# TensorE's routed-tile loop in turns of sixteen tiles instead of eight, with the first 32 tiles written out

## The reference

```python
x = x + attention(layernorm(x))      # 16 heads' width taken as one head of 1024, causal, scores / sqrt(1024)
h = layernorm(x)                     # 4096 tokens, D = 128
scores = softmax(h @ gate_w.T)       # E = 8 experts
top_scores, sel = top_k(scores, 2)   # each token goes to K = 2 experts
y = silu(h @ w1[e]) * (h @ w3[e]) @ w2[e]   # H = 256, per chosen expert e
x = x + sum over the two choices of score * y
```

## Time and profile before

| what | value |
|---|---|
| median of 3 runs | 320.21 us (319.2 to 321.56) |
| the profiled execution | 322.9 us, of which 321.1 us are the span of the trace |
| routed tiles | from 146 us to 307 us of the span |
| TensorE matmuls busy | 249.1 us (78%) |
| VectorE busy | 205.8 us (64%) |
| GpSimd busy | 181.8 us (57%) |
| mean granted TensorE clock | 0.925 of full speed |

### The profile page before, as it was taken

One profiled execution on the slowest core, in us unless ns is written; L12 is line 12 of the kernel. 1 busy time (PEld: TensorE's weight loads), 2 busy tenths in 40 slices (PEclk: granted clock), 3 DMA queues, 4 the chain that ended last, 5 costly groups with the idle time before them and its releaser, 6 DMA issues.

```text
span 321.1 us, 5987 instructions
## 1 busy us (share of the span) xinstructions
PE 249.1 (78%) x1619; PEld 202.1 (63%) x1620; DVE 205.8 (64%) x944; ACT 127.7 (40%) x348; POOL 181.8 (57%) x230
## 2 busy tenths in 40 slices
PE   0788999989798979875949433998998989888900
PEld 0766788869566768573837322877776778677700
DVE  1758988654897547674738213976766767689705
ACT  1155656463564535271326101434434444334400
POOL 4379933737687825618554774555555555455630
PEclk9999999999999979999778755999999999999965
DMA  7953500101001100104112211244332223567436
GB/s 235 324 168 95 166 2 1 44 25 36 26 34 53 47 15 26 42 2 111 43 52 64 70 58 42 70 107 103 83 82 79 74 75 106 175 197 210 141 108 216
DMA packets 31145, 28.94 MB, mean 90 GB/s; under 512 B 4360, under 2 KB 25872, under 8 KB 31120
## 3 DMA queue, kind: packets, MB, share of 16 engines
q1 hardware_dynamic: 25168, 18.81, 21.2%
q0 software_dynamic: 4352, 9.05, 8.4%
q10 hardware_dynamic: 1600, 0.79, 0.8%
HBM read 16.40 MB, written 12.22 MB: 89 GB/s over the span
## 4 chain that ended last, share of the span: by engine, by line
PE 58%; issue 8%; another core or an unknown queue 8%; DVE 8%; SPq 5%; ACT 5%; DMA 4%; POOL 3%; POOLq 0%; DVEq 0%
PE weighed L586 7%; PE scores L625 6%; PE scores L533 6%; PE mixed L648 6%; PE turned L634 5%; PE scores L627 5%; PE weighed L648 5%; PE turned L560 5%; PE scores L626 5%; PE scores L617 2%; DMA ysb<-L_ffn_w 2%; PE mixed L547 2%; ACT Pr L751 2%; SPq L290 1%
## 5 line engine op out<-in xcount | busy, mean ns | idle before, releaser
L444 POOL DMA_INDIRECT choice_rows<-ysb,ydest x72 | 70.1, 974 | 57.7 <-DVE ysb L1027 36.5
L435 POOL DMA_INDIRECT expert_rows<-rows,slots x64 | 63.1, 986 | 22.0 <-issue 16.6
L757 ACT ACTIVATE sil<-scores 128x256 f32<-128x256 f32 x72 | 27.7, 385 | 83.9 <-PE scores L627 62.7
L625 PE MATMUL scores<-W,xTh 128*128 x72 | 35.9, 499 | 13.0 <-issue 8.2
L586 PE MATMUL weighed<-TL,PT 128*128 128x128 f32 x288 | 39.2, 283 | 2.6 <-DVE X L837 1.6
L1007 DVE CAST xTh<-scores 128x128 fp32r<-128x128 f32 x72 | 20.7, 287 | 32.0 <-PE scores L617 19.0
L634 PE MATMUL turned<-identf,g 128*128 128x128 f32 x144 | 30.0, 292 | 11.8 <-DVE g L1017 8.7
L586 PEld LDWEIGHTS weighed<-TL,PT 128*128 128x128 f32 x288 | 35.7, 197 | 3.0 <-issue 2.9
L533 PE MATMUL scores<-XX,TL 128*128 128x512 f32 (+3 forms) x96 | 36.9, 493 | 0.8 <-ACT TL L737 0.7
L388 POOL TENSOR_TENSOR rstd<-ve,halves 128x1 f32<-128x1 f32 x32 | 19.8, 618 | 28.5 <-DVE ve L850 28.2
L762 ACT ACTIVATE gTs<-turned 128x256 f32<-128x256 f32 x72 | 27.6, 383 | 16.5 <-PE turned L634 12.3
(11 more groups left out here) (138 smaller groups left out, 531.9 us busy)
## 6 DMA issues: line engine op xcount, KB each, us to landing
xt<-expert_rows SPq DMA_DIRECT2D x72, 66.0 KB
XX<-choice_rows SPq DMA_DIRECT2D x16, 256.0 KB
ysb<-L_ffn_w SPq DMA_DIRECT2D x16, 128.0 KB, 2.2
choice_rows<-ysb,ydest POOLq DMA_INDIRECT x72
X<-L_attn_in_features SPq DMA_DIRECT2D x2, 512.0 KB, 8.8
expert_rows<-rows,slots POOLq DMA_INDIRECT x64
out<-X SPq DMA_DIRECT2D x4, 256.0 KB
expert_rows<-padrows SPq DMA_DIRECT2D x1, 528.0 KB
```

What stands on the lines that cost most here:

```text
L435: nc.gpsimd.indirect_dma_start(xs, bass.IndirectOffsetOnAxis(ap=slots[:, u, k:k + 1], axis=0), rows[:, u % ROWS_RING, k, :], None).then_in ...
L444: nc.gpsimd.indirect_dma_start(yb, bass.IndirectOffsetOnAxis(ap=ydest[:, q:q + 1], axis=0), ysb[:, q, :], None).then_inc(y_out[q], 16)
L625: mm(bank[2 + j % 2], xTh[:, j % 2, :], hi, start=True, stop=False)
L757: copy(sil[:, j % 2, :], bank[2 + j % 2][:, 0:H], ACT.Silu).then_inc(sil_rdy, 1)
```

## The change

`weights_of`, `step` and its parts take a turn number r and a place q of 0 to 15 in place of m and j of 0 to 7. TensorE's program becomes: a load of 18 entries (16 and the two before them), tiles 0 to 7, the wait for `place_rdy`, tiles 8 to 15 with the same registers, a load and tiles 16 to 31 written out, the wait for `list_rdy` 2, a loop of two turns of sixteen (32 to 63), and a load of 10 entries with tiles 64 to 71 written out. So there are five loads instead of nine, at tiles 0, 16, 32, 48 and 64; the loads at 8, 24, 40 and 56 are gone, and of six loop turns two are left. The matmuls, their order and the counts waited for stay as they are; the other engines' programs are the same.

```diff
-            def turn_x(m, j):
-
-                pe.wait_ge(xt_in[j], 16 * (m + 1))
+            def turn_x(r, q):
+
+                j, rounds = q % LANES, OUT_LANES // LANES
+                pe.wait_ge(xt_in[j], r * (16 * rounds) + 16 * (q // LANES + 1))
                 nc.tensor.transpose(bank[j % 2][:, 0:P], xt[:, j, 0:D], identf[:, :]).then_inc(xT_mm, 1)
 
-            def up(m, j, w):
-
-                t = m * LANES + j
-                pe.wait_ge(xT_rdy, t + 1)
+            def up(r, q, w):
+
+                pe.wait_ge(xT_rdy, r * OUT_LANES + q + 1)
 
                 hi, lo = W13[:, ds(w * UP, 2 * H)], W13[:, ds(w * UP + 2 * H, 2 * H)]
-                mm(bank[2 + j % 2], xTh[:, j % 2, :], hi, start=True, stop=False)
-                mm(bank[2 + j % 2], xTh[:, j % 2, :], lo, start=False, stop=False)
-                mm(bank[2 + j % 2], xTl[:, j % 2, :], hi, start=False, stop=True).then_inc(h_mm, 1)
-
-            def turn_g(m, j):
-
-                t = m * LANES + j
-                pe.wait_ge(g_rdy, t + 1)
+                mm(bank[2 + q % 2], xTh[:, q % 2, :], hi, start=True, stop=False)
+                mm(bank[2 + q % 2], xTh[:, q % 2, :], lo, start=False, stop=False)
+                mm(bank[2 + q % 2], xTl[:, q % 2, :], hi, start=False, stop=True).then_inc(h_mm, 1)
+
+            def turn_g(r, q):
+
+                pe.wait_ge(g_rdy, r * OUT_LANES + q + 1)
                 for c in range(H // P):
-                    i = nc.tensor.transpose(bank[4 + j % 2][:, c * P:(c + 1) * P], g[:, j % 2, c * P:(c + 1) * P],
+                    i = nc.tensor.transpose(bank[4 + q % 2][:, c * P:(c + 1) * P], g[:, q % 2, c * P:(c + 1) * P],
                                             identf[:, :])
                 i.then_inc(gT_mm, 1)
 
-            def down(m, j, w):
-                t = m * LANES + j
+            def down(r, q, w):
+                t = r * OUT_LANES + q
                 pe.wait_ge(gT_rdy, t + 1)
-                if isinstance(m, int) and m == 0:
+                first_eight = isinstance(r, int) and t < LANES
+                if first_eight:
 
                     wait(pe, y_rdy, t)
                     if t == 0:
                         pe.wait_ge(x1_rdy, N_TILES)
 
                 for c in range(H // P):
-                    i = mm(product_bank(m, j)[:, 0:D], gTs[:, j % 2, c * P:(c + 1) * P],
+                    i = mm((pO if first_eight else bank[6 + q % 2])[:, 0:D], gTs[:, q % 2, c * P:(c + 1) * P],
                            w2_sb[:, ds(w + c * D, D)],
                            start=c == 0, stop=c == H // P - 1)
                 i.then_inc(y_mm, 1)
 
-            def weights_of(m):
+            def weights_of(r, n):
 
                 _, w = nc.values_load_multi_w_load_instructions(
-                    wcol[0:1, ds(m * LANES, LIST0 + LANES)], engines=[pe.engine], min_val=0,
+                    wcol[0:1, ds(r * OUT_LANES + LIST0 - 2, n + 2)], engines=[pe.engine], min_val=0,
                     max_val=(E - 1) * WIDE, skip_runtime_bounds_check_because=IN_RANGE)
                 return w
 
-            def step(m, j, w):
-
-                static, t = isinstance(m, int), m * LANES + j
-                m_is_0 = static and m == 0
-                up(m, j, w[LIST0 + j])
-                if m_is_0 and has_xx(N_TILES + j):
-                    transposes(N_TILES + j)
+            def step(r, q, w):
+
+                def of(q):
+                    return r + q // OUT_LANES, q % OUT_LANES
+                static, t = isinstance(r, int), r * OUT_LANES + q
+                ending = static and t < LANES
+                up(r, q, w[2 + q])
+                if ending and has_xx(N_TILES + t):
+                    transposes(N_TILES + t)
                 if not static or t + 2 < NT:
-                    turn_x(m + (j + 2) // LANES, (j + 2) % LANES)
+                    turn_x(*of(q + 2))
                 if not static or t >= 1:
-                    turn_g(m + (j - 1) // LANES, (j - 1) % LANES)
+                    turn_g(*of(q - 1))
                 if not static or t >= 2:
-                    down(m + (j - 2) // LANES, (j - 2) % LANES, w[LIST0 + j - 2])
-                if m_is_0 and has_tl(N_TILES + j):
-                    projections(N_TILES + j)
-                if m_is_0 and group_at(N_TILES + j, RANK_LAG) is not None:
-                    ranks(group_at(N_TILES + j, RANK_LAG))
+                    down(*of(q - 2), w[q])
+                if ending and has_tl(N_TILES + t):
+                    projections(N_TILES + t)
+                if ending and group_at(N_TILES + t, RANK_LAG) is not None:
+                    ranks(group_at(N_TILES + t, RANK_LAG))
+
+            def steps(r, n=OUT_LANES):
+                w = weights_of(r, n)
+                for q in range(n):
+                    step(r, q, w)
+                return w
 
             for s in range(1 - XT_LEAD, N_TILES):
                 if s > 1 - XT_LEAD:
...
                 if is_tile(s - PV_LAG):
                     weigh(s - PV_LAG)
             pe.wait_ge(list_rdy, 1)
-            w = weights_of(0)
+            w = weights_of(0, OUT_LANES)
             weigh(N_TILES - 1)
             pe.wait_ge(w_in, 16)
             pe.wait_ge(split_lo, E)
             turn_x(0, 0)
             turn_x(0, 1)
-            for j in range(LANES):
-                step(0, j, w)
+            for q in range(LANES):
+                step(0, q, w)
             pe.wait_ge(place_rdy, NG)
-            w = weights_of(1)
-            for j in range(LANES):
-                step(1, j, w)
-            with pe.Fori(2, M0) as m:
-                w = weights_of(m)
-                for j in range(LANES):
-                    step(m, j, w)
+            for q in range(LANES, OUT_LANES):
+                step(0, q, w)
+            steps(1)
             pe.wait_ge(list_rdy, 2)
-            with pe.Fori(M0, M_TILES - 1) as m:
-                w = weights_of(m)
-                for j in range(LANES):
-                    step(m, j, w)
-            w = weights_of(M_TILES - 1)
-            for j in range(LANES):
-                step(M_TILES - 1, j, w)
-            turn_g(M_TILES - 1, LANES - 1)
-            for j in range(LANES - 2, LANES):
-                pe.wait_ge(y_rdy, NT - LANES + j - 1)
-                down(M_TILES - 1, j, w[LIST0 + j])
+            with pe.Fori(NT0 // OUT_LANES, NT // OUT_LANES) as r:
+                steps(r)
+            last, n = NT // OUT_LANES, NT % OUT_LANES
+            w = steps(last, n)
+            turn_g(last, n - 1)
+            for q in range(n - 2, n):
+                pe.wait_ge(y_rdy, NT - n + q - 1)
+                down(last, q, w[2 + q])
 
 
         @block.scalar
```

More of the change, by code:

```diff
@@ L259, in xx_bank @@
             return pS[s % 2][:, 512:] if xx_apart(s) else pM[:, :]
+        assert NT0 == 2 * OUT_LANES and NT % OUT_LANES == LANES
         LAST_SLOT = N_TILES - 1 + PLACE_LAG
```

## The result

The change made the kernel slower: 341.3 us median (341.0 to 342.2) against 320.3 (319.2 to 321.6), ratio 1.0645, 95% interval 1.0593 to 1.0698. The prediction, 319.9 us with a range up to 322.8, was wrong. The profiled execution took 341.0 us, its span 339.2 us, 18.1 more than before.

The account below looks back on a forecast made before the run. TensorE was taken as the bound between tiles 16 and 56, its idle time lost. Removed turn starts gained 1.8 us, longer loads at the remaining starts lost 1.5: 0.3 less, from 320.2 to 319.9 us, range 316.8 to 322.8.

Parts of the forecast that it names:

- The price of a load: TensorE's weight loads: 18 entries cost 1.41 us, 0.47 more than 12, bounds 0 and 0.62; tile 64's 10 entries 0.16 less.
- the likeliest case: Whole kernel: gains and losses nearly cancel, 0.3 us less, 319.9 us, own range 317.1 to 321.3, chance 0.72.
- The sequencer's part of a start: TensorE's register instructions in written-out tiles: fewer needed, costed at nothing, up to 0.5 us gained in the range.
- The removed starts: Loads dropped at tiles 8, 24, 40 and 56: gains of 0, 1.0, 0.8 and 0 us, sum 1.8.
- Tile 8's gain: Removed start at tile 8: time gained is waited for later at GpSimd's burst; 0, bounds 0 and 0.56 us gained.
- The branch back found its instructions: Rival at tile 48: the taken branch must refetch instructions; chance 0.14, two blocks 323.5 us (0.10), one block about 322.
- the window of two blocks: Skill page's rule on TensorE's loop: branches outside two 256-instruction blocks stall; about 2 us a block, up to 4.
- every late first tile comes back: Rival at tiles 8, 24, 40, 56: removed starts return all lateness, 4.8 us; net 3.3 less, 316.9 us, chance 0.14.
- that rival's 1.8: Tile 40's share of the gain if removed turn starts return all their first tile's lateness: 1.8 us; chance 0.14.
- 0.10 for slower: Whole kernel: chance 0.10 of over 1% slower, from two instruction blocks fetched at tile 48's branch, 323.5 us.

Follow-up runs that it names:

- b_written: The kernel before with its two loops written out, the same nine loads of 12 entries and no branch; 274.8 us, ratio 0.994 (0.991 to 0.997).
- a20_aligned: The change with loads of 20 entries (last 12) from a multiple of 16 entries; 276.6 us, ratio 1.002 to the kernel before.
- b12_shift2: The kernel before with LIST0 = 6 and every 12-entry load begun 8 bytes off its boundary; 306.2 us (1 run) where the kernel before takes 276.
- a_warm: The change with 28 unused transposes queued ahead of the loads at tiles 16, 32, 48 and 64; 340.7 us (one run), 6.1% above the kernel before.
- the last three runs: a_warm, plus later early fetches and additions, once with all tiles written out and short hidden loads (319.8 us), once in the kernel before (322.8 us).
- before_again: The kernel before, unchanged, run again on a chip where it takes about 276 us; 277.6 us (1 run).

## Why the prediction was wrong

*The price of a load* is the step that failed. "By proportion to 12 entries, 18 cost 1.41 us, 0.47 more", bounds 0 and 0.62: measured were 3.6 more for 18 entries and 1.6 more for 10, where 0.16 less was put down. The nearest rows, loads of 12 and 8 entries, all start on a multiple of 8 entries, and `LIST0 - 2` in the diff was read as a number of entries and not as an address. Even for aligned entries proportion was no law: 20 took 1.43 us and 18 took 1.77, where 12 took 0.95, so 18 cost 0.8 us more and the upper bound of 0.62 was too low as well.

The Trainium skill, page "Runtime: NRT & Kernel Launch", section "Instruction fetch mechanics", gives about 200 ns a register for a TENSOR_LOAD from device memory, "even for bulk". The prediction cited that section for another rule and passed this one by. The moved loads here, from on-chip memory, agree with it roughly (250 to 260 ns an entry), the aligned ones do not (71 to 122 ns). By it 18 entries are 3.6 us, an estimate. It would have made a rival, not the likeliest case: by the same figure 12 entries are 2.4 us, and the trace before had them at 0.94.

*A term was missing.* Nothing in the sum said that TensorE's clock falls behind a longer pause. At tile 32 the two tiles behind it came 1.6 us later than at full clock, and the `weigh` behind the first load took 1.7 us more. Over the starts of tiles 16, 32, 48 and 64 the first tiles came 11.2 us later than in the trace before, and the two tiles behind each 5.9 us in all.

*The sequencer's part of a start.* "I cost this at nothing", the prediction says of the register instructions, with 0.5 us in the range. b_written shows that with the branch they make up most of a start's lateness, 0.5 to 0.9 us at each of the starts of tiles 24 to 56. This did not decide the result.

*The removed starts.* On a chip at 276 us, where nothing else is late, the periods at tiles 24, 40 and 56 went from 2.54, 2.29 and 2.33 us to 1.47. These are 1.1, 0.8 and 0.9 us; predicted were 1.0, 0.8 and 0 to 0.2, the last from a trace in which a late matmul covered the load. Tile 8's gain was given back within seven tiles (tiles 8 to 15 took 30.2 us in the profile after, 29.7 before), as predicted. a20_aligned, the change without its moved start, is within 1% of the kernel before, as forecast, but in part by luck: the removed starts gave 2.8 us and not 1.8, its four later starts left took 1.2 us more, and 0.9 us went at tile 57 (2.39 us after tile 56, where it was 1.49).

*The rivals.* The branch back found its instructions: the last transfer on the queue ahead of it came at 268 us, the branch at 272.2 took 0.24 us, and the second turn fetched nothing; so a body of some 400 instructions does stay on the chip, and the window of two blocks, on which this rival rested, does not show. That every late first tile comes back did not show clearly: in the profile after tile 40 follows after 1.47 us instead of 3.23, all of that rival's 1.8, but tiles 24 and 56 after 1.89 and 2.29 instead of 2.50 and 2.80, and other tiles are late in their place (43 and 46 after 2.42 and 2.46). The rival that came true, a load slow for its address, was not among them, so 0.10 for slower was too little: a new form of an instruction that no row shows was bounded by rows of a form that differed in more than size.

*Where the 18.1 us of span are.* From the first load to tile 0: 9.5 us against 4.6, 4.9 more. From tile 15 to 71: 111.3 against 98.9, 12.3 more. The first load began 0.9 us later, in a stage that is the same. Tiles 0 to 15 and what comes behind tile 71 took the same as before. Sum 18.1.

## What to carry to other kernels

What a register load costs depends more on where it starts than on how many entries it takes: begin it on a 16-byte boundary, and take one or two entries too many rather than start between boundaries. Where a change alters an address, a count and a length at once, look for a row for each; a duration from rows that share all three bounds nothing. A stall of TensorE costs more than its length once the granted clock falls. Short loads of four entries, issued right behind the three matmuls of `up`, cost nothing here: the tiles stayed 1.47 to 1.48 us apart. When a turn's start is late, count the branch and the register instructions too, and write the loop out once to see their part.

## What the runs showed of the hardware

- TENSOR_LOAD from on-chip memory on TensorE's sequencer: 4, 10, 12, 18 and 20 aligned entries took 0.33, 1.2, 0.95, 1.8 and 1.4 us (medians); 12 and 18 entries from 8 bytes off took 3.1 and 4.5 to 4.6, and 10 took 2.5 and 3.1 in two loads.
- After idling for 3.93 us, on two chips, TensorE's matmuls ran at 1.2 GHz (0.50) in the next two tiles, in part or throughout. After 2.3 to 2.8 us of idling the clock fell in eight cases (b12_shift2 at tiles 16, 24, 40 and 56, a_warm at 32 and 48, the change at 64 on two chips) and stayed at 2.4 GHz (1.00) in three (b12_shift2 at tiles 32 and 48, a_warm at 16).
- A taken branch back took 0.21 to 0.24 us on TensorE's sequencer, one not taken 0.08; a loop body of some 400 instructions was run again with no instruction transfer.
- The same program took 276 us on two chips and 320 to 321 us where the change and the last three runs were measured. Of the 45 us between the spans of the kernel before (321.1) and before_again (275.9), 9 lie ahead of the first load, 25 between tiles 0 and 15 and 10 between tiles 15 and 71; the cause is open.
